# A four-block network on one core: 128-partition gates, owners and biases, and a new instruction order on every engine

## The reference

```python
# block 1, RWKV: time mixing, then channel mixing
k, v, r = xk @ Wk, xv @ Wv, xr @ Wr                     # 128 -> 512; xk, xv, xr mix a token with the one before it
wk, wkv = scan over time of exp(min(k, 60)) and exp(k) * v
x = x + (sigmoid(r) * wkv / wk) @ Wo
x = x + sigmoid(xr @ cm_Wr) + silu(xk @ cm_Wk) @ cm_Wv
# block 2, soft tree: 255 gates, 256 leaves
ret = leaf_probs(sigmoid(q @ routers.T)) @ leaf_values @ Wout + b
# block 3, causal attention: 16 heads of 8 numbers, rotary positions
out = softmax(q k / sqrt(8) + mask) v @ Wo
# block 4, mixture of experts: 16 routed, 2 shared
s = softmax(u @ centroids.T + expert_biases); g = the two largest, the rest 0
return u + sum_e g_e * (u @ Wr_e.T + br_e) + shared(u)
```

## Time and profile before

| | |
|---|---|
| time, median of 3 runs | 2122.94 us (2122.04 to 2125.04) |
| time of the profiled execution | 2123.6 us |
| its span | 2121.8 us |
| mean granted TensorE clock | 0.91 |
| PE busy | 1803.8 us (85%) |
| DVE busy | 1556.5 us (73%) |
| ACT busy | 1008.4 us (48%) |
| POOL busy | 926.7 us (44%) |

### The profile page before, as it was taken

The page is one execution under the profiler, slowest core; times in us unless marked ns, Lnnn a source line. Parts: engine busy times, 40 slices in busy tenths (PEclk is TensorE's granted clock), DMA queues, the critical chain, the costliest instruction groups (busy, mean ns, idle before and its releaser), DMA issues.

```text
span 2121.8 us, 33790 instructions
## 1 busy us (share of the span) xinstructions
PE 1803.8 (85%) x12141; PEld 1110.8 (52%) x12141; DVE 1556.5 (73%) x3386; ACT 1008.4 (48%) x1997; POOL 926.7 (44%) x1160
## 2 busy tenths in 40 slices
...
GB/s 90 1 5 45 1 20 33 7 45 12 46 12 45 1 44 14 12 46 12 46 12 46 12 46 1 25 33 12 45 12 45 12 46 1 43 9 10 43 12 6
DMA packets 64617, 53.34 MB, mean 25 GB/s; under 512 B 6019, under 2 KB 63171, under 8 KB 64451
## 3 DMA queue, kind: packets, MB, share of 16 engines
...
## 4 chain that ended last, share of the span: by engine, by line
PE 37%; DVE 37%; ACT 12%; issue 6%; POOL 4%; DMA 3%; SPq 1%; ACTq 0%; DVEq 0%; POOLq 0%
PE bank L870 34%; DVE rmax L741 10%; DVE wkb L688 4%; DVE ksum L675 4%; DVE tree L651 4%; PE bank L866 4%; ACT prob L462 3%; DMA qh<-maxT 3%; DVE kvsum L680 2%; DVE prob L821 2%; DVE rmax L738 2%; POOL rstd L341 2%; DVE stats L642 2%; DVE kvb L651 1%; ACT xd L468 1%
## 5 line engine op out<-in xcount | busy, mean ns | idle before, releaser
L462 ACT ACTIVATE prob<-bank 128x512 f32<-128x512 f32 x640 | 353.8, 594 | 132.5 <-PE bank L870 123.1
L741 DVE TENSOR_REDUCE rmax<-bank 128x1 f32<-128x512 f32 (+2 forms) x768 | 351.5, 501 | 48.5 <-PE bank L870 48.1
L428 POOL TENSOR_TENSOR prob<-xdT,spread 128x512 f32<-128x512 f32 x128 | 162.2, 1267 | 393.3 <-ACT spread L462 393.3
L870 PE MATMUL bank<-qh,kh 75*128 75x512 bf16 (+3 forms) x1024 | 270.0, 318 | 67.0 <-ACT prob L462 44.9
L870 PE MATMUL bank<-kh,qh 72*128 72x512 bf16 (+3 forms) x1024 | 279.0, 320 | 31.1 <-DVE rmax L741 13.6
L462 ACT ACTIVATE spread<-bank 128x512 f32<-128x512 f32 x128 | 76.4, 597 | 476.2 <-PE bank L870 476.2
L870 PE MATMUL bank<-wexpT,prob 128*128 128x128 f32 x2048 | 288.8, 285 | 0.0
L870 PEld LDWEIGHTS bank<-wexpT,prob 128*128 128x128 f32 x2048 | 255.3, 195 | 35.5 <-issue 24.0
L870 PEld LDWEIGHTS bank<-qh,kh 75*128 75x128 bf16 x1024 | 103.6, 101 | 254.9 <-ACT prob L462 176.5
L688 DVE RECIPROCAL wkb<-wkb 128x512 f32<-128x512 f32 x64 | 213.7, 3338 | 0.0
L870 PE MATMUL bank<-maskTb,identb 128*128 128x128 bf16 x1024 | 202.3, 228 | 0.0
...
## 6 DMA issues: line engine op xcount, KB each, us to landing
...
```

The source lines that it names most:

```text
L428: raised(pool.tensor_tensor(ug[:, e % 4, :], xdT[:, :], spread[e // 2 % 2][:, :], ALU.mult), "ug_side")
L462: raised(act.activation(dst, src, func, **kw), signal)
L741: last = dve.tensor_reduce(rmax[:, j, h:h + 1], S[n % 2][:, col:col + (j + 1) * P], AX_X, ALU.max)
L870: return pe.matmul(out_, w, x, start=start, stop=stop, **kw)
```

## The change

Two things change together.

The first is the width of some operands. `gT`, `owner`, `brow_part`, `bias_rows` and `ones_rows` get 128 partitions. All but `ones_rows` are zeroed once at the start by POOL, and the real rows are the same as before. The bf16 parts of the maxima and of the gates move into `max_cols` and `gate_cols`, whose reads now take 128 columns (the 48 real ones and 80 that lead to rows nobody reads).

The second is the order of all five lists. The rows of batch b no longer start the turn after the routing of batch b-1. They start earlier, right after `xn2T` of batch b+1, and lie between the steps of the channel mixing, the routing and the experts.

```diff
     sp="""
-        7:heads 7:max_rows 5:load 9:store
+        2:heads 0:load 2:max_rows 4:store
     pe="""
-        1:v0 3:row0 3:row1 2:gates0 3:row2 3:row3 2:gates1 3:row4 4:gT 3:row5 3:row6 4:gb0 1:k0 4:biases 3:row7 3:row8 4:gb1 3:row9 4:gb2 3:row10
...
-        3:weigh14 3:weigh15 1:cmk0 1:cmk1 3:back1 1:cmk2 3:attT 1:cmk3 3:attn_out 1:cmr 1:cmv 3:xdT 0:xnT 3:centroids 3:shared 1:xbT
+        3:maxT 4:expert12 4:expert13 4:expert14 1:k2 4:expert15 3:score0 3:score1 1:r2 3:score2 3:score3 1:v2 3:score4 3:score5 2:leafT0 3:score6 3:score7
+        2:leafT1 3:score8 3:score9 3:weigh0 3:score10 3:weigh1 3:score11 3:weigh2 2:leaf_sum 3:score12 3:score13 3:weigh3 3:score14 3:score15 1:v3
+        3:score16 3:score17 1:k3 3:score18 3:score19 3:weigh4 3:weigh5 3:score20 3:weigh6 3:score21 2:xcT 3:score22 1:r3 3:score23 3:weigh7 2:rope0
...
+        3:score32 2:attn_v 3:score33 3:score34 3:score35 3:score36 3:score37 3:back0 3:score38 3:score39 3:weigh12 3:weigh13 3:weigh14 3:weigh15
+        1:read_out 3:back1 3:attT 3:attn_out 1:xn2T 2:row0 3:xdT 2:row1 2:row2 3:centroids 1:cmk0 2:row3 2:row4 1:cmk1 1:cmk2 2:row5 2:row6 1:cmk3 2:row7
+        3:shared 1:cmr 2:row8 1:cmv 2:row9 3:gT 2:row10 3:gb0 2:row11 2:row12 3:gb1 0:xnT 3:biases 2:row13 3:gb2 2:row14 3:expert0 3:gb3 2:row15 2:row16
+        3:expert1 2:row17 3:gb4 2:row18 3:expert2 3:gb5 2:row19 1:xbT 3:gb6 2:row20 3:expert3 0:k0 2:row21 2:row22 1:gates0 0:v0 2:row23 1:gates1 2:row24
...
+        2:row32 2:row33 3:gb11 3:expert9 2:row34 2:row35 3:gb12 3:expert10 2:row36 2:row37 2:row38 3:gb13 2:row39 3:gb14 3:expert11 3:gb15 0:r1
     dve="""
+        3:rowmax14 1:mix0 3:rowmax15 3:rowmax16 4:u4 3:rowmax17 1:mix1 3:rowmax18 3:rowmax19 1:mix2 3:rowmax20 0:moments0 3:rowmax21 1:clamp0 3:rowmax22
...
+        3:max_parts 1:wkv0 2:tree5 1:ksum0 2:tree6 1:clamp2 1:kv1 2:tree7 4:yd 1:ksum1 4:moments7 1:inverse0 1:kvsum1 1:kv2 1:wkv1 2:yb 2:moments4
+        1:inverse1 1:clamp3 1:kvsum2 1:wkv2 1:ksum2 1:ksum3 2:rope_mul0 2:rope_mul1 2:rope_mul2 1:kv3 2:rope_mul3 1:inverse2 1:kvsum3 1:wkv3 1:inverse3
+        3:attend0 3:attend1 1:x2 1:moments2 3:yc 3:moments6 2:rowmax0 1:mix3 1:mix4 2:rowmax1 2:rowmax2 3:route_logits 2:rowmax3 1:silu0 2:rowmax4 1:silu1
+        3:route_probs 2:rowmax5 3:largest0 1:silu2 2:rowmax6 3:others 1:silu3 3:largest1 3:gates 2:rowmax7 0:moments1 2:rowmax8 1:y0 2:rowmax9 2:rowmax10
+        3:u0 2:rowmax11 1:moments3 2:rowmax12 3:u2 2:rowmax13
@@ operands
-        brow_part = sb("brow_part", [PARTS * NE, PARTS, P], BF16)
-        owner = sb("owner", [PARTS * NE, NE], BF16)
+        brow_part = sb("brow_part", [P, PARTS, P], BF16)
+        owner = sb("owner", [P, NE], BF16)
-        bias_rows, ones_rows = sb("bias_rows", [PARTS, T], BF16), sb("ones_rows", [PARTS, P], BF16)
+        bias_rows, ones_rows = sb("bias_rows", [P, T], BF16), sb("ones_rows", [P, P], BF16)
-        max_part = sb("max_part", [P, J, PARTS, NH], BF16)
+        max_cols, gate_cols = (sb(n, [P, (J - 1) * PARTS * NH + P], BF16) for n in ("max_cols", "gate_cols"))
-        gT = sb("gT", [PARTS * NE, T], BF16)
+        gT = sb("gT", [P, T], BF16)
@@ pool, at the start
+                      gT[:, :], owner[:, :], brow_part[:, :, :], bias_rows[:, :], max_cols[:, :], gate_cols[:, :])
@@ dve, at the start: the wait for the zeroed tiles comes before the first step instead of the fifth
+            dve.wait_ge(setup["ident"], 6)
@@ pe
-                    last = mm(G[0:PARTS * NH, j * P:(j + 1) * P], max_part[:, j, :, :].rearrange("p i h -> p (i h)"), identb[:, :])
+                    last = mm(G[:, j * P:(j + 1) * P], max_cols[:, j * PARTS * NH:j * PARTS * NH + P], identb[:, :])
-                    last = mm(G[0:PARTS * NE, j * P:(j + 1) * P], gate_part[:, j, :, :].rearrange("p i e -> p (i e)"), identb[:, :])
+                    last = mm(G[:, j * P:(j + 1) * P], gate_cols[:, j * PARTS * NE:j * PARTS * NE + P], identb[:, :])
-                raised(mm(G, owner[:, e:e + 1].broadcast_to([PARTS * NE, P]), gT[:, :]), "gb_ps")
+                raised(mm(G, owner[:, e:e + 1].broadcast_to([P, P]), gT[:, :]), "gb_ps")
```

More of the change, by code:

```diff
@@ L51 @@
     sp="""
-        7:heads 7:max_rows 5:load 9:store
+        2:heads 0:load 2:max_rows 4:store
     """,
     pool="""
-        1:root1 2:res 2:cmr_sig 4:root6 2:cmr_sum 2:root3 4:gate_rest 4:gate_lo 4:u1 4:u3 4:u5 4:u7 1:wk0 4:u9 1:r_sig0 4:u11 4:u13 2:root4 2:root_rms
-        4:u15 1:r_sig1 1:wk1 1:gated0 1:rwkv0 2:rope_sum0 2:rope_sum1 2:rest0 1:r_sig2 1:gated1 1:rwkv1 2:rest1 1:wk2 1:gated2 1:wk3 1:rwkv2 1:r_sig3
-        1:gated3 1:rwkv3 4:root7 2:part_lo0 0:root0 2:part_lo1 1:root2 0:x1_gain 0:x1_bias
+        4:u5 4:u7 4:u9 0:root0 4:u11 1:r_sig0 4:u13 4:u15 1:gated0 1:wk0 1:r_sig1 1:wk1 4:root7 1:rwkv0 1:gated1 2:root4 2:root_rms 1:r_sig2 1:rwkv1 1:wk2
@@ L58 @@
+        1:gated2 1:wk3 1:r_sig3 2:rope_sum0 2:rope_sum1 2:rest0 2:rest1 2:part_lo0 1:gated3 2:part_lo1 1:rwkv2 1:rwkv3 1:root2 3:root6 1:res 0:x1_gain
+        0:x1_bias 1:cmr_sig 1:cmr_sum 3:gate_rest 3:gate_lo 0:root1 3:u1 1:root3 3:u3
     """,
     act="""
-        4:xdT_out 1:mix_before0 1:mix_before1 4:route_exp 1:mix_before2 2:norm3 2:xbT_out 4:gate_hi 2:gate0 4:gate_mid 2:gate1 4:gT_out 4:spread1 1:k_exp0
-        4:spread3 1:r_tanh0 4:spread5 1:k_first0 4:spread7 4:spread9 4:spread11 2:leafT_out0 2:leafT_out1 4:spread13 1:k_exp1 3:vaug 4:spread15 1:k_first1
@@ L62 @@
[L62 to L65, removed]
@@ L66 @@
-        1:cmk_tanh2 3:attT_out 1:cmk_tanh3 1:cmr_tanh 0:norm1 3:norm6
+        2:cmr_tanh 4:gate_hi 4:gate_mid 4:gT_out 1:norm1 4:spread1 1:mix_before0 1:mix_before1 1:mix_before2 4:spread3 2:norm3 4:spread5 2:xbT_out 3:vaug
+        1:k_exp0 2:gate0 1:k_first0 2:gate1 4:spread7 1:r_tanh0 4:spread9 4:spread11 4:spread13 4:spread15 3:maxT_out 1:k_exp1 1:r_tanh1 1:k_first1 3:exp0
+        3:exp1 3:exp2 3:exp3 1:k_exp2 3:exp4 3:exp5 3:exp6 3:exp7 2:leafT_out0 3:exp8 2:leafT_out1 3:exp9 4:norm7 3:exp10 3:exp11 1:k_first2 3:exp12
@@ new lines @@
+        3:exp13 1:r_tanh2 3:exp14 3:exp15 3:exp16 3:exp17 3:exp18 3:exp19 2:norm_rms 3:exp20 3:exp21 2:xcT_out 1:k_exp3 3:exp22 3:exp23 1:k_first3 3:exp24
+        3:exp25 1:r_tanh3 3:exp26 3:exp27 3:exp28 3:exp29 2:part_hi0 2:part_hi1 3:exp30 3:exp31 2:part_mid0 3:exp32 3:pvT_out0 3:exp33 3:exp34 2:part_mid1
+        3:exp35 3:exp36 3:exp37 3:exp38 3:exp39 3:pvT_out1 2:norm4 3:attT_out 1:norm2 3:norm6 1:mix_before3 1:mix_before4 3:xdT_out 0:norm0 1:cmk_tanh0
+        3:route_exp 1:cmk_tanh1 1:cmk_tanh2 1:cmk_tanh3 2:values
@@ new lines @@
+        4:u6 1:kv0 3:rowmax23 1:kvsum0 2:tree0 3:rowmax24 3:rowmax25 2:tree1 4:u8 3:rowmax26 2:tree2 3:rowmax27 3:rowmax28 2:tree3 3:rowmax29 2:tree4
+        3:rowmax30 3:rowmax31 4:u10 3:rowmax32 3:rowmax33 1:clamp1 3:rowmax34 4:u12 3:rowmax35 3:rowmax36 3:rowmax37 3:rowmax38 3:rowmax39 4:u14
+        3:max_parts 1:wkv0 2:tree5 1:ksum0 2:tree6 1:clamp2 1:kv1 2:tree7 4:yd 1:ksum1 4:moments7 1:inverse0 1:kvsum1 1:kv2 1:wkv1 2:yb 2:moments4
+        1:inverse1 1:clamp3 1:kvsum2 1:wkv2 1:ksum2 1:ksum3 2:rope_mul0 2:rope_mul1 2:rope_mul2 1:kv3 2:rope_mul3 1:inverse2 1:kvsum3 1:wkv3 1:inverse3
@@ L80 @@
[L80 to L87, removed]
```

20 lines of the change are left out of this document (11 added, 9 removed).

## The result

| | before | changed |
|---|---|---|
| median of 4 runs | 2123.57 us (2122.04 to 2125.04) | 2102.58 us (2096.08 to 2103.91) |
| profiled execution, its span | 2123.6, 2121.8 us | 2096.1, 2094.2 us |
| granted TensorE clock, mean | 0.91 | 0.90 |
| PE busy, DVE busy | 1803.8, 1556.5 us | 1725.3, 1591.4 us |

A forecast was written before the change was run, and what follows sets the result against it. The period bounds the kernel, through the loop of heads, R, M and S: 17.2 + 54.5 + 4.9 + 37.8 = 114.4 us. Span 203 + 106 + 14 x 114.4 + 136 = 2046.6, so 2048 us; range 2002 to 2110.

The forecast's parts named there:

- filling: Time before batch 0's first row: 203 us, as the chain before those rows now comes later; 223.4 us before batch 1 today.
- Gap: From `score39` to the next `row0`: 17.2 us instead of 23.3, with the DMAs of `heads` as the last wait.
- M and S: M, in which the maxima are moved, stays 4.9 us; S, the scores, goes from 38.7 to 37.8 us.
- R: The stretch from `row0` to `maxT`: from 50.8 us to 54.5, bounds 51.5 and 58.
- DVE's part of R: DVE's work from `row0` to `maxT`: 48.6 + 3.2 - 0.5 = 51.3 us.
- the operands: Switching to 48-row operands and back costs PE 0.17 us; wide ones save 19 x 0.17 = 3.2 us from `row0` to `maxT`.
- the friction: From `row0` to `maxT`, 2.2 us more than either engine's work, as today, added to the engines' sums.
- The clock: One 6.7 us half-clock spell from `row0` to `maxT`, from PE's wait for DMAs, costing up to 3.4 us of PE's work.
- The moved work eats the gap: Rival, 0.16: `row0` to `maxT` grows to 57.4 us, the period stays 117.3, only filling and draining shorten: 2089 us.
- The rival of PE's clock: Rival, 0.15: half clock for three spells from `row0` to `maxT`, PE's part 6.7 us longer, period 121.1, time 2142 us.
- Everything that was slack comes back: Rival, 0.19: `row0` to `maxT` stays at 51.5 us, PE catches up, period 111.2, time 2004 us.
- the sign of a wrong kind: Granted clock below 0.9 from `row0` to `maxT`, `row0` waiting for `xn2T` or `read_out`, or unchanged spacing around `gb`.

The follow-up runs named there:

- Experiment 4: The changed kernel without the 18 head DMAs of batches 1 to 15 (wrong heads, only its time counts): 2063.36 us, ratio 0.973.
- experiment 8: The changed kernel with spare constant matmuls at six places on PE and `rowmax7` ahead of `gates` in DVE's list: 2040.68 us, ratio 0.9621.
- experiment 1: The changed kernel with the order of the kernel before, so the wide operands alone: 2124.45 us, ratio 1.0022.
- experiment 11: The changed kernel with spare constant matmuls at six places on PE, two before `row0` and four between rows 9 and 12: 2047.28 us, ratio 0.9654.
- 6: The kernel before with the new order and its narrow operands, plus spare constant matmuls at six places on PE: 2092.77 us, ratio 0.9859.
- experiment 7: The changed kernel with `rowmax7` ahead of `gates` in DVE's list: 2089.83 us, ratio 0.985.
- experiment 2: The kernel before with the order of the changed one and its own narrow operands: 2226.45 us, ratio 1.0496.
- 5: The changed kernel with only the `gb` matmuls back on 48 partitions: 2190.28 us, ratio 1.0289.

## Why the prediction was wrong in size

Direction and range held, the size didn't. By its own steps:

| term | forecast | measured |
|---|---|---|
| filling | 203 | 197.4 |
| first period | 106 | 110.0 |
| 14 periods | 1601.6 | 1645.8 |
| draining | 136 | 141.0 |

The span is 47.6 us above the forecast, and 44 of them lie in the periods. The ends were off both ways, filling 5.6 too long and the other two 9.0 too short, which nearly cancels. No experiment looks at them.

**Gap: right.** 17.2 forecast, 16.8 measured, and ended by the DMAs within a microsecond of their landing. Experiment 4 confirms that 13.5 us stand behind them.

**M and S: right to within 0.7 us.** M 4.7 for 4.9, S 38.5 for 37.8. S was to lose 2.1 us with its half-clock spell. The spell did go (S of batch 7 has the clock at 1.00, it was 0.94), but S stayed as long as before.

**DVE's part of R, the operands, the friction: near.** 51.3 forecast, 52.05 measured in the changed kernel, of which `hots` has 1.1, and 51.24 in experiment 8. The spacing around `gb` changed as forecast. The weight loads of 128 columns didn't grow. The operands were worth nothing in the old order (experiment 1) and 2.7 us in the new with the clock held (11 against 6), for 3.2 forecast. By the prediction's own terms and without half clock R would be DVE's 51.3 + 2.2 = 53.5. Experiments 8 and 11, with the clock held, have 53.8 and 54.1.

**The clock: the step that failed.** "I put one whole spell into R, at a price of half its length, up to 3.4 us of PE's work." In the sum this gave R only 1.0 us (54.5 - 53.5), as DVE was nearly as full and hid the rest. Measured were 11.8 us at half clock in R of batch 7, in two spells (11.0 on average), and giving the clock back by spare matmuls shortened R by 3.9 us (experiment 11). I took the length of the spell from today's rows, 6.7 us. But the new order leaves PE with 9.6 us of work in the 16.6 of the gap, where it had 20.3 in 23.9, and makes the first rows, at half clock, the fuller list: 8.40 of 8.40 us for PE, 5.45 for DVE. PE's debt there isn't caught up, since both engines are near their sum in the rest of R.

In the prediction's own sum, 11.0 us at half clock give PE 48.4 + 3.8 - 3.2 + 5.5 = 54.5, and R 56.7 with the 2.2 of friction. That is 2.2 of the 3.5 us by which R was missed. Of the other 1.3, `hots` explains 0.7 (experiment 7).

The reason given for the spell was wrong too. It was put down to the wait of `row0` for the DMAs, but the clock fell before that wait began (in 11 of 12 gaps), and it fell without that wait in experiment 4. What the rows show in front of the fall is the thin chain to `xn2T`. The reading of the earlier trace rows, that both of today's spells follow the idling in the gap, holds for the second only: the first begins at 1015.0, 4.3 us before the gap, when PE waits 1.5 us for ACT amid the scores.

**What was missing: `hots`.** It adds about 1 us of DVE time per period (1191 against 215 ns). Moving it gives 0.7 us of R, and 7 against the changed kernel is 12.8 us by the medians, 11 by the ratios, though those two intervals overlap by a hair.

**The rivals.** The period is that of "The moved work eats the gap": R 58.0 for its 57.4, the period the same as before. Its reason was wrong: neither did the operands give nothing, nor is there a fixed blocking through two banks, as R falls to 54 with the clock held. The rival of PE's clock had the mechanism, but I priced it at three spells alone, 20 us at half clock, and gave that 0.15. The 11.0 measured lie between that and the 6.7 of the forecast, a case that no rival had. The mean clock of R is 0.905, just above the 0.9 that was named as the sign of a wrong kind. Its bound, R above 59.9, was crossed only with narrow operands (experiments 2 and 5). "Everything that was slack comes back" fell: no version has R at 51.5.

**Open.** Why narrow operands keep the clock down longer in the new order (601 against 408 us in all) is not known. The rows only show that they do, and that spare matmuls on 128 partitions remove most of it (232). In the old order it is the other way round, 385 us with the narrow operands and 407 with the wide ones, so width alone is no answer. Nor is it known why the spell in the rows, between 24 and 38 us behind `row0` in experiment 2, comes after 13.6 us in which PE was busy for 12.1.
